# Two graph attention layers on one core: the fourth head's row copied into a PSUM bank, a bias addition a slot earlier, and two inverts moved

## The chip, the cores and the metric

The kernel runs on one core of a Trainium2 chip. The metric is the device time of one execution in microseconds, lower is better. TensorE (PE in the profile) multiplies matrices and writes PSUM only; VectorE (DVE), ScalarE (ACT) and GpSimd (POOL) work elementwise; SyncE (SP) issues the DMA transfers. Each engine works through its own queue in order, and semaphores hold the queues together.

## The reference

There are 16 graphs of 512 nodes with 256 features each, and an adjacency matrix for each. Every graph goes through this:

```python
mask = (adj > 0) | eye(N)
def gat_layer(x, W, a_src, a_dst, bias):      # H heads of F features
    xl = x @ W
    e = leaky_relu(asrc[:, None] + adst[None, :], 0.2)   # source and target scores of each head
    attn = softmax(where(mask, e, -1e9), over sources)
    return attn.T @ xl + bias
h = elu(gat_layer(x, W1, ...))        # layer 1: 4 heads of 128, concatenated
h = gat_layer(h, W2, ...)             # layer 2: one head of 256
x = layernorm(x + h)
Wh = x @ W3                           # layer 3: scores e[i, j] from Wh, masked, softmax over i
x = layernorm(x + leaky(attention @ Wh))
```

## The kernel before, in words

The nodes of a graph (called a batch here) lie in four blocks of 128 partitions. The work of a batch is cut into units: four heads of layer 1 (kind "h", index 0 to 3), layer 2 ("L2") and layer 3 ("L3"). A software pipeline takes one unit per slot and six slots (`SLOTS`) per batch: slot g is slot pos = g % 6 of batch n = g // 6. Position 0 holds layer 3 of batch n-3, positions 1 to 4 the four heads of batch n, position 5 layer 2 of batch n-1. The last layer 3 units come behind the loop. Each engine's block has the same loop over g, and the order of its queue is written out by hand there; nothing plans it.

A unit passes through these steps, over several slots:

- `tops` (line 983, VectorE) finds for each target the greatest source score under the mask, as four calls of 128 x 512, one per block of targets. It adds the transposed mask `mask_t` (bfloat16, SBUF) and the row of source scores, the same on all partitions, and takes the maximum. For the heads of batches from 2 on (`by_dma`) this row is `a_rows[:, index]` in SBUF, which SyncE spreads by DMA (`spread_scores`, 341). For other units TensorE writes it into PSUM bank `bA` (`sources_row`, 514), where it waits for the maxima of the bank's user before (`u.ahead`).
- `shifted_targets` (996, VectorE) makes from the maxima the column `b_t`, in two operations of 128 x 4, `low` (1005) and `b_t` (1010).
- `targets_row` (525, TensorE) spreads b_t over bank bB, as the matmuls of L511.
- `leaky` and `exps` (ScalarE) write the weights into `att`; `keep_edges` (1032, VectorE) takes out the missing edges, in place.
- `attend` (601, TensorE) multiplies by the values, in two halves. It is issued in the slot behind that of its unit.
- `invert` (1020, VectorE) waits for each half of a head's attention and takes the reciprocals of the sums, `normalize` (802, ScalarE) scales with them, `elu_exp` (811, ScalarE) and `elu` (1013, VectorE, tile y) do the elu. TensorE turns y, ScalarE takes its high part, and `low_part` (1027, VectorE, tile y_lo) the rest.

Beside the units run the values of batch n+1 (`values_1`, whose input x_lo is VectorE's, line 1051), the values of layers 2 and 3, the layer norms, and the masks. GpSimd does the bias of layer 2 (`add_bias_2`, 440, 128 x 1024, in slot pos 3, behind the fourth head's b_t), the last residual (`residual_2`, 462, 128 x 1024), the diagonal of the mask (`set_diag`, 456) and the scalings of the last norm (`norm_2`, 425, four of 128 x 256), each for some batch of the pipeline.

In VectorE's loop (line 1226 on) a slot's order is: invert the head of two slots before, maxima and targets of the next unit, the extras of the position, keep_edges of this unit, low part of the head of three slots before, elu of the head of two slots before.

Of the kernel before, what the change touches and what calls it, by code (L numbers as in the profile page):

```python
# [10 lines left out]
ALU = mybir.AluOpType  # L11
# [3 lines left out]
LOWEST = -3.0e38  # L15
# [5 lines left out]
SLOTS = 6  # L21


class Unit:


    def __init__(self, kind, batch, index, slot):
        self.kind = kind
        self.batch = batch
        self.index = index  # L30
        self.slot = slot
        self.row = kind != "L3"

        self.by_dma = kind == "h" and batch >= 2


def gat_kernel(nc, x, adj, W1, as1, ad1, b1, W2, as2, ad2, b2, W3, a3, out):
    B, N, D = x.shape
    HF = W1.shape[1]
    H, F = as1.shape  # L40
# [31 lines left out]
        u.u = i  # L72
    for i, u in enumerate(u for u in units.values() if u.row):
        u.r = i
    spreading = [u for u in units.values() if not u.by_dma]
    for i, u in enumerate(spreading):
        u.a, u.ahead = i, spreading[i - 1] if i else None

    pieces = 0
    for u in units.values():  # L80
# [9 lines left out]
    with ExitStack() as ctx:  # L90
# [6 lines left out]
        def sem(name):  # L97
            return ctx.enter_context(nc.semaphore(name))
# [124 lines left out]
        x1t_ready = sem("x1t_ready")  # L223
        val3_ready = sem("val3_ready")
        exp3_done = sem("exp3_done")
        act3_ready = sem("act3_ready")

        mask_made = sem("mask_made")
# [65 lines left out]
        def a_col(u, b):  # L294
            if u.kind == "h":
                c = HC + u.index % 2
                return val1[u.batch % 2][:, b, u.index // 2, c:c + 1]
            return val2[:, b, 0:1] if u.kind == "L2" else val3[u.batch % 2][:, b, 0:1]
# [16 lines left out]
        def _(sp):  # L315
# [25 lines left out]
            def spread_scores(n):  # L341

                sp.wait_ge(a_stored, 16 * H * (n - 1))
                for h in range(H):
                    if n > 2:
                        sp.wait_ge(top_done, (units[SLOTS * (n - 1) + 1 + h].u + 1) * NB)
                    sp.dma_start(a_rows[:, h], a_dram[h].rearrange("(o n) -> o n", o=1).to_broadcast([P, N]))\
                        .then_inc(a_spread[h], 16)

# [48 lines left out]
        def _(pool):  # L398
# [18 lines left out]
            def norm_scale(m, which, moments_sem, var_sem, rstd_sem):  # L417
                pool.wait_ge(moments_sem, (m + 1) * NB)
                nc.gpsimd.tensor_scalar(var_eps[:, which], moments[:, which, :, 1], EPS, 1.0, ALU.add, ALU.mult)\  # L419
                    .then_inc(var_sem, 1)  # L420
                pool.wait_ge(var_sem, m + 1)
                nc.gpsimd.tensor_tensor(rstd[:, which], var_eps[:, which], neg_half[:], ALU.pow).then_inc(rstd_sem, 1)
                pool.wait_ge(rstd_sem, m + 1)
# [16 lines left out]
            def add_bias_2(m):  # L440
                if m == 0:
                    pool.wait_ge(bias2_ready, 1)
                pool.wait_ge(x_loaded[m % 4], (m // 4 + 1) * 16)
                pool.wait_ge(xt_turned, (m + 1) * KD)
                nc.gpsimd.tensor_tensor(x_in[m % 4][:], x_in[m % 4][:], bias2[:].unsqueeze(1).to_broadcast([P, NB, DO]),
                                        ALU.add).then_inc(xb_done, 1)
# [23 lines left out]
            for g in range(LAST):  # L470
                n, pos = divmod(g, SLOTS)
                if pos == 0 and 0 <= n - 3:
                    scale_3(n - 3)
                if pos == 2 and 0 <= n - 2 < B:
                    norm_scale(n - 2, 0, moments1, var1, rstd1)
                if pos == 2 and 0 <= n - 2 < B:
                    pool.wait_ge(x1n_done, (n - 1) * NB)
                if pos == 2 and 0 <= n - 3 < B:
                    residual_2(n - 3)
                if pos == 2 and 0 <= n + 1 < B:  # L480
                    set_diag(n + 1)
                if pos == 3 and 0 <= n - 1 < B:

                    pool.wait_ge(b_t_ready, units[SLOTS * n + H].r + 1)
                    add_bias_2(n - 1)
                if pos == 4 and 0 <= n - 3:
                    norm_2(n - 3)
            add_bias_2(END)
# [284 lines left out]
        def _(act):  # L773
# [43 lines left out]
            def high_part(u):  # L817
# [2 lines left out]
                    act.wait_ge(val2_done, u.batch * NB)  # L820
                nc.scalar.copy(y_hi[:, u.index], bU[u.turn_use % 4][:]).then_inc(y_hi_ready, 1)

            def x_out(n):
                for k in range(KD):
                    act.wait_ge(xt_turned, n * KD + k + 1)
                    nc.scalar.copy(x_hi[:, k], g_bank(k)).then_inc(x_hi_ready, 1)
# [64 lines left out]
            for g in range(LAST + 1):  # L891
                n, pos = divmod(g, SLOTS)
                if n == 0:
                    first_heads(g)
                    continue
                this, older, oldest = units.get(g), head_at(g - 2), head_at(g - 3)
                third, second, batch = 0 <= n - 2 < B, 0 <= n - 1 < B, 0 <= n + 1 < B
                third_layer = units.get(g - 2) if pos == 2 else None
                if this:
                    leaky(this, (0, 1))  # L900
                if third_layer:
                    third_out(third_layer, 0)
                if older:
                    normalize(older)
                if pos == 5 and n + 2 < B:
                    x_out(n + 2)
                if pos == 0 and batch:
                    values_1_out(n + 1, 0)
                if this:
                    leaky(this, (2, 3))  # L910
                if pos == 2 and batch:
                    values_1_out(n + 1, 3)
                if pos == 3 and second:
                    values_2_out(n - 1, (2, 3))
                if pos == 4 and third:
                    values_3_out(n - 2, (0, 1))
                if this:
                    exps(this)
                if pos in (0, 1) and batch:
                    values_1_out(n + 1, pos + 1)  # L920
                if third_layer:
                    third_out(third_layer, 1)
                if pos == 2 and second:
                    values_2_out(n - 1, (0, 1))
                if pos == 3 and third:
                    x1_out(n - 2)
                if oldest:
                    high_part(oldest)
                if pos == 4 and third:
                    values_3_out(n - 2, (2, 3))  # L930
                if older:
                    elu_exp(older)
# [41 lines left out]
        def _(dve):  # L974
# [7 lines left out]

            def tops(u):

                if u.by_dma:
                    dve.wait_ge(a_spread[u.index], 16 * (u.batch - 1))
                else:
                    dve.wait_ge(arow_done, u.a + 1)
                if u.kind == "h" and u.index == 0:
                    dve.wait_ge(mt_loaded, (u.batch + 1) * NB * 16)  # L990
                for b in range(NB):
                    nc.vector.tensor_tensor_reduce(junk[:, b] if u.row else att[u.slot % 3][:, b], mask_t[u.batch % 4][:, b],  # L992
                                                   a_rows[:, u.index] if u.by_dma else bA[:], 1.0, a_col(u, b) if u.row else LOWEST, ALU.add, ALU.max,
                                                   top[u.u % 2][:, b:b + 1]).then_inc(top_done, 1)

            def shifted_targets(u):
# [130 lines left out]

            def tops_by_targets(u):

                dve.wait_ge(arow_done, u.a + 1)  # L1130
                for b in range(NB):
                    col = slice(b, b + 1)
                    nc.vector.tensor_tensor_reduce(att[u.slot % 3][:, b], mask_t[u.batch % 4][:, b], bA[:], 1.0, LOWEST,
                                                   ALU.add, ALU.max, top[u.u % 2][:, col]).then_inc(top_done, 1)
                    dve.wait_ge(top_done, u.u * NB + b + 1)
                    nc.vector.scalar_tensor_tensor(low[:, col], top[u.u % 2][:, col], -1.0, b_cols(u)[:, col], ALU.mult, ALU.max)\
                        .then_inc(low_done, 1)
                    dve.wait_ge(low_done, u.u + b + 1)
                    nc.vector.scalar_tensor_tensor(b_t3[:, col], top[u.u % 2][:, col], TOP, low[:, col], ALU.subtract,
                                                   ALU.min, reverse0=True).then_inc(b_t3_ready, 1)  # L1140
# [85 lines left out]
            for g in range(LAST + 1):  # L1226
# [3 lines left out]
                    continue  # L1230
                this, after, older, oldest = units.get(g), units.get(g + 1), head_at(g - 2), head_at(g - 3)
                last_head = head_at(g - 4) if pos == 2 else None
                if older and older is not final_head:
                    invert(older)
                if g == LAST:
                    tops(thirds[END - 2])
# [19 lines left out]
                    norm_stats(n - 3, 1, res2, res2_done, 2, stats2, moments2)  # L1256
                if this and this.row:
                    keep_edges(this)
                if oldest and pos != 1:
                    low_part(oldest)  # L1260
                if older:
# [63 lines left out]
```

## Time and profile before

| | |
|---|---|
| median of 3 runs | 930.41 us (929.71 to 932.02) |
| profiled execution | 932.84 us, of which the span of the trace is 930.9 |
| TensorE busy | 852.8 us, 92% of the span |
| VectorE busy | 785.3 us, 84% |
| ScalarE busy | 689.8 us, 74% |
| GpSimd busy | 294.4 us, 32% |
| mean granted TensorE clock | 0.989 of full speed |
| chain that ended last | PE 50%, DVE 27%, ACT 13%, issue 9% |

A timeline row gives the start in us from the span's start, the duration in us, the engine, the line of the kernel, the operation, the tile written and those read, their shapes, and the count of merged instructions. Brackets at its end give how long the engine was idle before it and what released it ("issue" where the profile shows no one). Starts and ends of successive instructions overlap a little, since they are pipelined. Buffer numbers are left out of tile names: `att` is one of three.

### The profile page before, as it was taken

To read this page: it belongs to the slowest core of one execution; us is meant where nothing else is said; L and a number is where in the kernel's file an instruction comes from. 1 tells how busy PE (TensorE), PEld (TensorE's weight loads), DVE (VectorE), ACT (ScalarE), POOL (GpSimd) and SP (SyncE) were. 2 spreads that over 40 slices of the span, in tenths; PEclk is the share of its full clock that TensorE was granted. 3 is DMA by queue.
4 is the path that set the end of the run, shared out by engine and by line. 5 is a ranking of instruction groups with operands and counts; after the bars stand their busy time and mean duration, and the time that the engine had idled before them with its cause. 6 is when DMAs were issued, how large, how long until landed. Compare 5 with 4: busy or idle time off the path is not lost.

```text
span 930.9 us, 16958 instructions
## 1 busy us (share of the span) xinstructions
PE 852.8 (92%) x5996; PEld 791.0 (85%) x5996; DVE 785.3 (84%) x1922; ACT 689.8 (74%) x1288; POOL 294.4 (32%) x244
## 2 busy tenths in 40 slices
PE   6787889999999999999999999999999999989986
PEld 5787779888989888898988889898888989879875
DVE  6766797989897998989899898989989898898666
ACT  2666759779686877968788796878879687797753
POOL 0000101234342623434262342326224242433512
PEclk9898999999999999999999999999999999999999
DMA  9122131311313131121313113231321311100002
GB/s 247 42 74 64 46 91 47 91 46 43 81 60 91 47 113 46 40 75 68 92 46 109 51 35 80 69 92 46 111 49 35 81 69 24 46 24 1 24 0 68
DMA packets 100378, 59.80 MB, mean 64 GB/s; under 512 B 66244, under 2 KB 84804, under 8 KB 100296
## 3 DMA queue, kind: packets, MB, share of 16 engines
q1 hardware_dynamic: 100296, 58.73, 23.1%
q8 instruction: 49, 0.80, 0.5%
q14 instruction: 33, 0.27, 0.2%
HBM read 41.82 MB, written 8.50 MB: 54 GB/s over the span
## 4 chain that ended last, share of the span: by engine, by line
PE 50%; DVE 27%; ACT 13%; issue 9%; another core or an unknown queue 0%; DMA 0%; POOL 0%; DVEq 0%; SPq 0%; POOLq 0%; ACTq 0%
PE bUU L573 10%; DVE junk L992 10%; PE bUU L562 8%; PE bG L645 8%; PE bG L663 8%; PE bUU L551 7%; DVE y L1017 4%; PE bB L511 3%; ACT x L807 3%; DVE y_lo L1029 2%; ACT att L780 2%; DVE stats L1082 2%; DVE att L1039 2%; ACT att L795 2%; ACT att L792 2%
## 5 line engine op out<-in xcount | busy, mean ns | idle before, releaser
L551 PE MATMUL bUU<-val,att 128*128 128x129 f32 x2048 | 249.4, 275 | 0.8 <-DVE att L1043 0.8
L551 PEld LDWEIGHTS bUU<-val,att 128*128 128x128 f32 x2048 | 241.3, 192 | 3.1 <-issue 1.3
L780 ACT ACTIVATE att<-bB,val 128x512 f32<-128x512 f32 x320 | 202.4, 704 | 5.2 <-PE bB L511 5.2
L1043 DVE SCALAR_TENSOR_TENSOR att<-mask_n,att 128x2048 f32<-128x2048 bf16 x64 | 153.6, 2399 | 50.9 <-ACT att L795 50.9
L992 DVE CUSTOM_DVE_ANT_0 junk<-mask_t,a_rows,val 128x512 bf16<-128x512 bf16 x224 | 189.7, 901 | 0.0
L562 PE MATMUL bUU<-val,att 128*128 128x257 f32 x480 | 113.2, 384 | 16.0 <-ACT x L807 13.1
L795 ACT ACTIVATE att<-att 128x2048 f32<-128x2048 f32 x64 | 123.4, 1929 | 0.6
L562 PEld LDWEIGHTS bUU<-val,att 128*128 128x128 f32 x480 | 87.8, 190 | 33.1 <-ACT x L807 18.8
L573 PE MATMUL bUU<-val3s,att 128*128 128x256 f32 x480 | 108.3, 379 | 0.2 <-DVE res L1073 0.2
L419 POOL TENSOR_SCALAR var_eps<-moments 128x4 f32<-128x4 f32 x29 | 32.3, 1115 | 235.8 <-DVE moments L1085 235.8
L807 ACT ACTIVATE x<-bUU,zinv 128x128 f32<-128x128 f32 x256 | 73.2, 369 | 45.1 <-DVE zinv L1023 45.1
L848 ACT COPY val<-bG 128x524 f32<-128x524 f32 x62 | 37.3, 602 | 87.2 <-PE bG L663 87.2
L573 PEld LDWEIGHTS bUU<-val3s,att 128*128 128x128 f32 x480 | 90.0, 190 | 12.3 <-DVE res L1073 0.6
L453 POOL TENSOR_SCALAR val3s<-val,z3inv 128x256 f32<-128x256 f32 x60 | 49.1, 832 | 137.8 <-DVE z3inv L1060 134.7
L511 PE MATMUL bB<-ident,b_t 128*128 128x128 f32 x320 | 51.4, 284 | 34.1 <-DVE b_t L1010 31.8
L645 PE MATMUL bG<-w_hi,y_hi 128*128 128x258 f32 x256 | 75.2, 294 | 0.3 <-DVE y_lo L1029 0.3
L511 PEld LDWEIGHTS bB<-ident,b_t 128*128 128x128 f32 x320 | 35.3, 139 | 44.6 <-DVE b_t L1010 42.1
L663 PE MATMUL bG<-w_hi,x_hi 128*128 128x262 f32 x248 | 72.7, 293 | 0.0
L663 PE MATMUL bG<-w_lo,x_hi 128*128 128x262 f32 x248 | 72.6, 293 | 0.0
L663 PE MATMUL bG<-w_hi,x_lo 128*128 128x262 f32 x248 | 72.5, 292 | 0.0
L645 PE MATMUL bG<-w_hi,y_lo 128*128 128x258 f32 x256 | 72.3, 282 | 0.0
L645 PE MATMUL bG<-w_lo,y_hi 128*128 128x258 f32 x256 | 72.2, 282 | 0.0
(127 smaller groups left out, 1743.5 us busy)
## 6 DMA issues: line engine op xcount, KB each, us to landing
adj_in<-in_adj_dram SPq DMA_DIRECT2D x16, 1024.0 KB, 5.9
a_rows<-a_rows_dram SPq DMA_DIRECT2D x56, 256.0 KB, 3.9
x_in<-in_x_dram SPq DMA_DIRECT2D x16, 512.0 KB, 6.7
out_dram<-act SPq DMA_DIRECT2D x14, 512.0 KB, 2.9
mask_t<-mask_n SPq DMA_TRANSPOSE x64, 2.5
a_rows_dram<-val SPq DMA_DIRECT2D x56, 2.0 KB
att<-in_L_gnn_W_dram SPq DMA_DIRECT2D x4, 128.0 KB, 3.2
val<-in_L_gnn_W_dram SPq DMA_DIRECT2D x1, 512.0 KB, 7.4
```

Source lines behind the costliest of these rows:

```text
L453: nc.gpsimd.tensor_scalar(val3s_of(m, b), val3[m % 2][:, b, 2:DX], z3inv[:, b:b + 1], 1.0, ALU.mult, ALU.mult)\
L511: ins = nc.tensor.transpose(bank[:, b * P:(b + 1) * P], column(b).to_broadcast([P, P]), ident[:])
L551: ins = nc.tensor.matmul(to[:, (d % 2) * FX:(d % 2 + 1) * FX], p[:, s, d * P:(d + 1) * P], val1[u.batch % 2][:, s, u.index // 2, values], ...
L562: ins = nc.tensor.matmul(to[:, 0:DO + 1], p[:, s, d * P:(d + 1) * P], val2[:, s, 2:DX + 1], start=(s == 0), stop=(s == NB - 1))
L573: ins = nc.tensor.matmul(to[:, d * DO:(d + 1) * DO], p[:, j, (2 * i + d) * P:(2 * i + d + 1) * P], val3s[:, j], start=(j == 0), stop=(j == ...
L645: ins = nc.tensor.matmul(g_bank(b % 2)[:, 0:DX], left[:, k, nodes], right[:, k], start=(k == 0 and i == 0), stop=(k == KH - 1 and i == 2))
L663: ins = nc.tensor.matmul(to, left[:, k, nodes], right[:, k, g], start=False, stop=(k == KD - 1 and i == 2))
L780: nc.scalar.activation(p[:, b], bB[:], ACT.Prelu, bias=a_col(u, b), alpha=SLOPE)\
L795: nc.scalar.activation(flat(p), flat(p), ACT.Exp).then_inc(exp_done, 1)
L807: nc.scalar.activation(x1[u.h % 2][:, d * P:(d + 1) * P], bU[u.use[d // 2] % 4][:, (d % 2) * FX:(d % 2) * FX + F], ACT.Copy, scale=zinv[u. ...
L992: nc.vector.tensor_tensor_reduce(junk[:, b] if u.row else att[u.slot % 3][:, b], mask_t[u.batch % 4][:, b], a_rows[:, u.index] if u.by_dma ...
L1043: nc.vector.scalar_tensor_tensor(flat(p), mask_n[u.batch % 3][:, 0:NB * N], BIG, flat(p), ALU.add, ALU.min)\
```

## The change

Three things change. First, the row of the fourth head (index 3) of batches from 2 on is copied from `a_rows` in SBUF into bank bA by ScalarE, in slot pos 2, between the leaky operations of the second head and the copy of the values of the next batch; VectorE's maxima read bA. The bank's order of users takes the fourth heads in, and SyncE waits for the copy, not for the maxima, before it spreads the next row over this part of `a_rows`. Second, GpSimd's bias addition moves from slot pos 3 to pos 2, between the scale of the first norm and the residual, and waits for the third head's b_t instead of the fourth's. Third, the inverts of the third and fourth heads no longer open the slots pos 5 and pos 0; they stand at the end of slots pos 4 and pos 5, behind keep_edges and ahead of the low part. The other inverts stay.

```diff
-        self.by_dma = kind == "h" and batch >= 2
+        self.by_dma = kind == "h" and batch >= 2
+        self.banked = self.by_dma and index == 3
@@
-    spreading = [u for u in units.values() if not u.by_dma]
+    spreading = [u for u in units.values() if not u.by_dma or u.banked]
     for i, u in enumerate(spreading):
         u.a, u.ahead = i, spreading[i - 1] if i else None
+        u.turned = len([v for v in spreading[:i] if not v.banked])
@@ SyncE, spread_scores
-                        sp.wait_ge(top_done, (units[SLOTS * (n - 1) + 1 + h].u + 1) * NB)
+                        if h == H - 1:
+                            sp.wait_ge(arow_copied, n - 2)
+                        else:
+                            sp.wait_ge(top_done, (units[SLOTS * (n - 1) + 1 + h].u + 1) * NB)
@@ GpSimd
                 if pos == 2 and 0 <= n - 2 < B:
                     norm_scale(n - 2, 0, moments1, var1, rstd1)
+                if pos == 2 and 0 <= n - 1 < B:
+                    pool.wait_ge(b_t_ready, units[SLOTS * n + 3].r + 1)
+                    add_bias_2(n - 1)
...
-                if pos == 3 and 0 <= n - 1 < B:
-                    pool.wait_ge(b_t_ready, units[SLOTS * n + H].r + 1)
-                    add_bias_2(n - 1)
@@ ScalarE
+            def row_into_bank(u):
+                act.wait_ge(a_spread[u.index], 16 * (u.batch - 1))
+                act.wait_ge(top_done, (u.ahead.u + 1) * NB)
+                nc.scalar.copy(bA[:], a_rows[:, u.index]).then_inc(arow_copied, 1)
...
                 if this:
                     leaky(this, (2, 3))
+                if pos == 2 and n >= 2:
+                    row_into_bank(units[g + 2])
                 if pos == 2 and batch:
                     values_1_out(n + 1, 3)
@@ VectorE, tops (tops_by_targets likewise waits for u.turned)
-                if u.by_dma:
+                if u.banked:
+                    dve.wait_ge(arow_copied, u.batch - 1)
+                elif u.by_dma:
                     dve.wait_ge(a_spread[u.index], 16 * (u.batch - 1))
                 else:
-                    dve.wait_ge(arow_done, u.a + 1)
+                    dve.wait_ge(arow_done, u.turned + 1)
...
-                                                   a_rows[:, u.index] if u.by_dma else bA[:], 1.0, ...
+                                                   a_rows[:, u.index] if u.by_dma and not u.banked else bA[:], 1.0, ...
@@ VectorE, the loop
-                if older and older is not final_head:
+                if older and older.index < 2 or g == SLOTS:
                     invert(older)
...
                 if this and this.row:
                     keep_edges(this)
+                if pos in (4, 5) and g < LAST - 1:
+                    invert(head_at(g - 1))
                 if oldest and pos != 1:
                     low_part(oldest)
                 if older:
                     elu(older)
```

## Rows read from the trace of the kernel before

**Rows 1.** Busy us by engine in one batch's stretch, with granted clock and DMA

```profile
400.40:454.90 54.50, 51.89 (x374) 48.48 (x373) 48.21 (x116) 42.69 (x81) 21.14 (x15) 1.00 0.24 68
```

**Rows 2.** TensorE's timeline: start, us, operation, [idle before, releaser]

```profile
417.00 0.65 PE L511 MATMUL bB<-ident,b_t 128*128 128x128 f32 x4 [1.10 <-issue]
...
425.32 0.65 PE L511 MATMUL bB<-ident,b_t 128*128 128x128 f32 x4 [0.60 <-DVE b_t L1010]
...
427.55 1.95 PE L551 MATMUL bUU<-val,att 128*128 128x129 f32 x16
...
429.34 0.60 PE L511 MATMUL bA<-ident,val 128*128 128x128 f32 x4
...
434.87 0.36 PE L660 MATMUL bG<-bias,ones_r 128*128 128x262 f32 x1
...
439.41 2.00 PE L562 MATMUL bUU<-val,att 128*128 128x257 f32 x8 [0.86 <-ACT x L807]
```

**Rows 3.** VectorE's timeline in the same stretch

```profile
403.98 0.16 DVE L1010 SCALAR_TENSOR_TENSOR b_t<-top,low 128x4 f32<-128x4 f32 x1
...
411.34 2.29 DVE L992 CUSTOM_DVE_ANT_0 junk<-mask_t,a_rows,val 128x512 bf16<-128x512 bf16 x1
...
413.56 1.63 DVE L992 CUSTOM_DVE_ANT_0 junk<-mask_t,a_rows,val 128x512 bf16<-128x512 bf16 x1
...
416.78 0.16 DVE L1010 SCALAR_TENSOR_TENSOR b_t<-top,low 128x4 f32<-128x4 f32 x1
...
416.86 2.29 DVE L1043 SCALAR_TENSOR_TENSOR att<-mask_n,att 128x2048 f32<-128x2048 bf16 x1
...
420.04 1.88 DVE L1017 SCALAR_TENSOR_TENSOR y<-e,x 128x512 f32<-128x512 f32 x1 [0.89 <-ACT e L815]
...
426.85 2.29 DVE L1043 SCALAR_TENSOR_TENSOR att<-mask_n,att 128x2048 f32<-128x2048 bf16 x1
...
429.66 0.68 DVE L1017 SCALAR_TENSOR_TENSOR y<-e,x 128x512 f32<-128x512 f32 x1
...
430.41 0.67 DVE L992 CUSTOM_DVE_ANT_0 att<-mask_t,bA 128x512 f32<-128x512 bf16 x1
...
433.50 1.22 DVE L1053 TENSOR_TENSOR x_lo<-bG,x_hi 128x1024 fp32r<-128x1024 f32 x1
...
434.99 2.36 DVE L1039 SCALAR_TENSOR_TENSOR att<-mask_n,att 128x1024 f32<-128x1024 bf16 x2 [0.27 <-ACT att L792]
...
441.61 0.16 DVE L1010 SCALAR_TENSOR_TENSOR b_t<-top,low 128x4 f32<-128x4 f32 x1
```

**Rows 4.** L992, the row maximum, by operands: ns min/median/max, first and last start

```profile
L992 DVE CUSTOM_DVE_ANT_0 junk<-mask_t,a_rows,val x224: 728/748/2289, 115.9 to 847.1; 128x512 bf16<-128x512 bf16 x112
...
L992 DVE CUSTOM_DVE_ANT_0 junk<-mask_t,bA,val x96: 720/739/748, 25.0 to 885.0; 128x512 bf16<-128x512 bf16 x96
```

**Rows 5.** GpSimd's timeline in the same stretch

```profile
410.68 2.39 POOL L467 TENSOR_TENSOR res<-act,x1n 128x1024 f32<-128x1024 f32 x1 [8.80 <-DVE x1n L1093]
...
413.04 1.60 POOL L459 TENSOR_TENSOR mask_n<-mask_n,ident_big 128x512 bf16<-128x512 bf16 x1
...
417.02 4.34 POOL L445 TENSOR_TENSOR x_in<-x_in,bias 128x1024 f32<-128x1024 f32 x1 [2.37 <-issue]
...
426.95 2.24 POOL L419 TENSOR_SCALAR var_eps<-moments 128x4 f32<-128x4 f32 x1 [5.59 <-DVE moments L1085]
...
430.41 4.84 POOL L428 TENSOR_SCALAR act<-res,moments,rstd 128x256 f32<-128x256 f32 x4
```

**Rows 6.** ScalarE's timeline in the same stretch

```profile
404.37 0.60 ACT L848 COPY val<-bG 128x524 f32<-128x524 f32 x1 [1.26 <-PE bG L663]
...
422.10 1.14 ACT L807 ACTIVATE x<-bUU,zinv 128x128 f32<-128x128 f32 x4 [0.93 <-DVE zinv L1023]
...
424.77 1.97 ACT L795 ACTIVATE att<-att 128x2048 f32<-128x2048 f32 x1
```

**Rows 7.** GpSimd's residual addition over the whole span, as in rows 4

```profile
L467 POOL TENSOR_TENSOR res<-act,x1n x13: 2372/2394/2397, 192.6 to 842.9; 128x1024 f32<-128x1024 f32 x13
```

More of the change, by code:

```diff
@@ L225, in gat_kernel @@
         exp3_done = sem("exp3_done")
+        arow_copied = sem("arow_copied")
         act3_ready = sem("act3_ready")
@@ L992, in tops @@
                     nc.vector.tensor_tensor_reduce(junk[:, b] if u.row else att[u.slot % 3][:, b], mask_t[u.batch % 4][:, b],
-                                                   a_rows[:, u.index] if u.by_dma else bA[:], 1.0, a_col(u, b) if u.row else LOWEST, ALU.add, ALU.max,
+                                                   a_rows[:, u.index] if u.by_dma and not u.banked else bA[:], 1.0, a_col(u, b) if u.row else LOWEST, ALU.add, ALU.max,
                                                    top[u.u % 2][:, b:b + 1]).then_inc(top_done, 1)
@@ L1128, in tops_by_targets @@
             def tops_by_targets(u):
-                dve.wait_ge(arow_done, u.a + 1)
+                dve.wait_ge(arow_done, u.turned + 1)
                 for b in range(NB):
```

## The prediction

> **What bounds the kernel now.** I read three kinds of view in this order: the busy time of one stretch, the engines' timelines over that stretch, and the durations of VectorE's row maximum by its operands. The stretch 400.4 to 454.9 us is one batch in the steady part, and TensorE is busy 51.9 of its 54.5 us at the full clock (1.00, 2.4 GHz), VectorE 48.2, ScalarE 42.7 [rows 1]. So TensorE is the bound, and a change can win only the time in which it stands still, unless it makes it stand still more. In the batch TensorE has three waits: 1.10 us before the targets' row of the fourth head (start 417.00), 0.60 before that of the second layer (425.32), 0.86 inside the second layer's attention (439.41) [rows 2]. The idle column counts from end to start, while groups that don't wait overlap by 427.55 + 1.95 - 429.34 = 0.16 us [rows 2], so each costs that much more: 1.27, 0.77 and 1.02. Beside them, TensorE's start at 434.87 follows VectorE's x_lo, done at 433.50 + 1.22 = 434.72 [rows 2, 3], so x_lo paces it there with no wait to speak of. The ceiling of any gain is therefore about 3.2 us a batch.
>
> The first wait is for the fourth head's b_t, which VectorE has done at 416.78 + 0.16 = 416.94 [rows 3]; the view calls its releaser "issue", but TensorE starts 0.06 us behind that. It is late because of the row maxima before it: the first took 2.29 and the second 1.63 us [rows 3], where the median of the form is 0.75 [rows 4]. Meanwhile GpSimd ran its residual addition (410.68 to 413.07) and the diagonal (413.04 to 414.64) [rows 5]. The maxima end when those end: one engine holds something and the other waits. The same is seen at 420.04, where the elu (y) took 1.88 against GpSimd's bias addition, which ended at 421.36, and that addition took 4.34 because keep_edges, 416.86 to 419.15, had started first [rows 3, 5].
>
> **The change part by part.** *The row in the bank.* The maximum from bank bA took 720 to 748 ns in all 96 cases, while the form from a_rows reaches 2289 [rows 4]. The third layer's first maximum, from bA as well, ran at 430.41 in 0.67 us under GpSimd's scalings, which began at the same 430.41 [rows 3, 5]. So the fourth head's maxima lose (2.29 - 0.75) + (1.63 - 0.75) = 2.4 us, and b_t comes at 414.5 (414.7 if its two small operations, which read SBUF twice, wait for the diagonal). TensorE is free at 417.00 - 1.27 = 415.73, so the first wait goes whole: TensorE 1.27 sooner. The other bank users stand in VectorE's own order, and bA is free: the third layer's maxima end by 434 of the batch before, the second layer's row needs it only after the fourth head.
>
> *ScalarE's copy.* It stands after the second head's leaky operations, and ahead of the copy at 404.37 ScalarE idles 1.26 us for TensorE [rows 6]. No row shows a copy from SBUF to PSUM. The nearest is that same copy of 524 columns from PSUM to SBUF, 0.60; from below it can't cost less than nothing, from above the exponential over four times as many columns, in SBUF alone, took 1.97 [rows 6]. I take 0.6, which the idle time hides; at 1.97 it would put 0.7 us a batch on ScalarE ahead of the second head's exponential. VectorE's new wait on it is over 7 us before the maxima at 411.34. SyncE's queue waits for the copy where it waited for the maxima, so the spreading of the next row is never later, and nothing behind it is.
>
> *GpSimd's bias a slot sooner.* It now starts at the third head's b_t, done at 403.98 + 0.16 = 404.14 [rows 3], and needs 4.34 less what it waited, 419.15 - 417.02, that is 2.3 us; it ends near 406.6. VectorE's next operation is keep_edges, which waits for ScalarE's exponential, and that starts some 0.5 behind the copy at 404.37 and takes 1.9, to 406.8 [rows 6]. So the bias lies in VectorE's idle time. Residual and diagonal follow at 410.68 as before. What it frees is y, which took 0.68 at 429.66: 1.88 - 0.68 = 1.20 us [rows 3].
>
> *What comes next in the batch.* TensorE's 1.27 brings x1 turned, ScalarE's copies and y's input 1.27 sooner; y starts at 418.77 and its end is 1.27 + 1.20 = 2.47 sooner. The second layer's maxima and b_t move with it, more than TensorE's 1.27 + 0.77, so the second wait goes too: TensorE 2.04 sooner. ScalarE's wait of 0.93 at 422.10 goes [rows 6]; it is then 1.27 + 0.93 and an overlap of 0.13 sooner, 2.33. So the fourth head's exponential ends at 424.77 + 1.97 - 2.33 = 424.41, and keep_edges runs 424.5 to 426.8 (before: 426.85 to 429.14 [rows 3]).
>
> *The inverts moved ahead.* For the third head VectorE now stands, behind keep_edges, until TensorE's attention is done: 427.55 + 1.95 - 2.04 = 427.46 [rows 2]. That is a new wait of 0.6 us, and low part, y and the third layer's maxima are queued behind it. The low part, an operation over as many columns as y, takes 0.6 to the start of the next, so y would start at 428.17. GpSimd's scalings start 430.41 - 429.14 = 1.27 us behind the end of keep_edges [rows 3, 5], so at 428.1. This is a near tie. I take it that GpSimd is first; y then waits for the first of four scalings, 4.84 / 4 = 1.21 us, until 429.2, and the third layer's maxima start at 429.8 instead of 430.41: 0.6 sooner. x_lo moves with them. TensorE had 2.04 and stands 1.4 us for x_lo. Behind x_lo, VectorE's wait of 0.27 for the exponential [rows 3] goes, so its work is 0.87 sooner from there.
>
> The fourth head's invert moves from behind two operations of 0.6 to ahead of them, which with the 0.87 is 2.1 us sooner; ScalarE's normalizing of the fourth head is then in time and the third wait, 1.02, goes. But TensorE's next need is the next batch's first b_t, at 441.61 + 0.16 = 441.77 before [rows 3], which VectorE brings 0.87 sooner. So TensorE stands once more, and the batch is 0.87 us shorter. From there TensorE leads to the fourth head again (ScalarE's idle time at 404.37 is such a wait), so nothing more is lost or won.
>
> **The sum.** The residual addition runs 13 times, from 192.6 to 842.9 [rows 7]: 13 batches have the collision. 13 x 0.87 = 11.3 us. The batches before them have no residual and no scalings; the new wait on the third head's invert and the earlier bias offset each other there, and I put them at nothing. The last batch, in which fewer things pace TensorE, may give a little more: 11.9 in all. Against the profiled execution (932.84, of which 930.9 is the span) that gives 920.9; the median of the runs shown is 2.4 lower, 930.41, and from it the forecast is 918.5 us.
>
> The one rule I weigh is that of the near tie. The rows show one wait of y that lasts to the end of one GpSimd operation, and a maximum that got in between residual and diagonal: the diagonal's 1.60 and the maximum's 1.63 took turns [rows 3, 5]. The Trainium skill, "SBUF — State Buffer", section "Who interferes with whom", says that a VectorE operation with two SBUF inputs and a GpSimd one that reads SBUF exclude each other for a whole instruction, and that issue order alone decides who waits. By that rule the tie's two ends are one scaling or none, never four; the first gives the sum above, the second the rival A below, and the rule speaks against rival B. The trace agrees with 1.88 for y.
>
> **The rivals.** *A, y is first at the tie.* Then the third layer's maxima start at 428.77, 1.64 sooner. GpSimd's scalings end later and may hold keep_edges of the second layer by some 0.5 us, so 1.4 a batch: 13 x 1.4 = 18.2, 912 us. For it: 0.07 us decides, and the tie may fall differently by batch. Against: the estimate of the tie itself.
>
> *B, VectorE does not get its turn between the four scalings (slower than before).* y, behind the new wait, stands for all 4.84 us, to 432.9; the third layer's maxima start near 433.5, 3.1 later than now, x_lo and TensorE with them; less the 0.27, 2.8 a batch, 13 x 2.8 = 36: 967 us. It decides from the point where y waits for more than 1.9 us, that is, where the maxima start after 430.41 + 0.27: with a second scaling, 1.2 more, the batch is 0.3 longer and the time 934. For it: the four have no wait between them. Against: the turn taken behind the residual.
>
> *C, the bank does not shield the maxima* (the change doesn't do what it says). Then the first wait stays, only y's 1.20 is won, and the invert's wait eats it: 930 us. Against: the 96 unslowed cases of [rows 4].
>
> *D, nothing stands behind the invert.* If the attention is done before keep_edges and the tie is won, TensorE itself is the limit and wins more of the 3.2 us a batch: 2.2 x 13 = 29, 902 us. Against: the third layer's maxima and targets, 433.50 - 430.41 = 3.1 us, stand ahead of x_lo [rows 3].
>
> **How the numbers follow.** The forecast has 0.50, A 0.25, B 0.07 (mostly its small form), C 0.10, D 0.08. The forecast and A hold three quarters, and the unknown copy could put up to 0.7 a batch, 9 us, on the forecast, with a small chance; so the range is 908 to 926. This kernel's measurement tells 0.3% from no change, 2.8 us, so faster means below 927.6: forecast, A and D nearly whole, 0.83. Within 0.3%: 0.10 (C and a dear copy). Slower: 0.07.
>
> **What would show it.** In the changed profile the fourth head's maxima should read bA and take 0.72 to 0.75 each; the bias addition should take 2.3 to 2.4 in every batch, and y at the fourth head's slot 0.68. TensorE's 1.10 and 0.60 waits should be gone, and the 0.86; in their place stand one of some 1.4 us before the L660 matmuls, released by x_lo, and one of some 0.9 before the first head's targets' row. The y under the scalings should take about 1.7. The distance of two residual additions should be 53.6 to 53.7 instead of 54.5. The forecast is wrong if ScalarE's copy takes over 1.26, if y there takes 0.68 (A) or over 3 (B), or if the first wait is still there (C).

## The result, and the profile after

The changed kernel took 906.6 us (median of 4 runs, 904.33 to 908.52) against 930.1 before: a ratio of 0.974 with a 95% interval of 0.972 to 0.977. It is faster by 2.6%, 23.5 us, about twice what I forecast, and 1.4 us below the low end of my range. The profiled execution's span is 904.3 us. One batch's stretch of it, with the columns of [rows 1]:

```profile
388.80:441.40 52.60, 51.21 (x373) 48.56 (x372) 44.47 (x114) 43.03 (x82) 17.83 (x15) 1.00 0.26 62
```

The view counts 373 matmuls where [rows 1] has 374, at the same clock, in a stretch 1.9 us shorter. VectorE is busy 3.7 us less: what has gone is time in which its operations stood under GpSimd. GpSimd, which stood as well, is busy 3.3 less.

The distance of the residual additions, seen over all 13 [rows 7], gives the mean batch between the first and the last of them: (842.9 - 192.6) / 12 = 54.19 us before, and after

```profile
L474 POOL TENSOR_TENSOR res<-act,x1n x13: 2393/2394/2406, 188.5 to 816.6; 128x1024 f32<-128x1024 f32 x13
```

(816.6 - 188.5) / 12 = 52.34. That is 22.2 us over 12 distances. The two profiled spans, 930.9 and 904.3, differ by 26.6, so 4.1 us of the profiles' difference lie ahead of the first residual addition (192.6 against 188.5) and 0.3 behind the last. In the steady batches the distance went from 54.5 to 52.6.

The batch that answers to the one shown before has its residual addition at 399.07 where [rows 5] has 410.68, so 11.61 is to be added to compare. TensorE's timeline at the places of [rows 2], in the new line numbers:

```profile
404.21 0.60 PE L518 MATMUL bB<-ident,b_t 128*128 128x128 f32 x4
...
411.71 0.60 PE L518 MATMUL bB<-ident,b_t 128*128 128x128 f32 x4
...
421.81 0.36 PE L667 MATMUL bG<-bias,ones_r 128*128 128x262 f32 x1 [0.65 <-DVE x_lo L1069]
...
423.60 3.63 PE L569 MATMUL bUU<-val,att 128*128 128x257 f32 x16
...
428.41 0.65 PE L518 MATMUL bB<-ident,b_t 128*128 128x128 f32 x4 [0.74 <-DVE b_t L1026]
```

The three waits of [rows 2] are gone: the targets' rows have no brackets, and the second layer's attention, which was cut in two by 0.86, is one row of 16. In their place stand the two that I forecast, one on x_lo and one on the next batch's first b_t, 0.65 and 0.74 where I had 1.4 and 0.9.

VectorE's timeline of the same batch:

```profile
399.82 0.73 DVE L1008 CUSTOM_DVE_ANT_0 junk<-mask_t,bA,val 128x512 bf16<-128x512 bf16 x1
400.47 0.74 DVE L1008 CUSTOM_DVE_ANT_0 junk<-mask_t,bA,val 128x512 bf16<-128x512 bf16 x1
...
402.80 0.16 DVE L1026 SCALAR_TENSOR_TENSOR b_t<-top,low 128x4 f32<-128x4 f32 x1
...
407.12 0.69 DVE L1033 SCALAR_TENSOR_TENSOR y<-e,x 128x512 f32<-128x512 f32 x1
...
412.78 2.29 DVE L1059 SCALAR_TENSOR_TENSOR att<-mask_n,att 128x2048 f32<-128x2048 bf16 x1
...
415.88 0.17 DVE L1039 RECIPROCAL zinv<-bUU 128x2 f32<-128x2 f32 x1 [0.73 <-PE bUU L558]
...
416.55 0.88 DVE L1033 SCALAR_TENSOR_TENSOR y<-e,x 128x512 f32<-128x512 f32 x1
417.35 0.67 DVE L1008 CUSTOM_DVE_ANT_0 att<-mask_t,bA 128x512 f32<-128x512 bf16 x1
...
420.45 1.21 DVE L1069 TENSOR_TENSOR x_lo<-bG,x_hi 128x1024 fp32r<-128x1024 f32 x1
421.59 2.34 DVE L1055 SCALAR_TENSOR_TENSOR att<-mask_n,att 128x1024 f32<-128x1024 bf16 x2
...
428.19 0.16 DVE L1026 SCALAR_TENSOR_TENSOR b_t<-top,low 128x4 f32<-128x4 f32 x1
```

The maxima from the bank take 0.73 and 0.74 although GpSimd's residual runs beside them, y at 407.12 takes 0.69 where [rows 3] had 1.88, and before the third head's invert VectorE stands 0.73 for TensorE, the new wait. GpSimd and ScalarE there:

```profile
392.71 2.37 POOL L452 TENSOR_TENSOR x_in<-x_in,bias 128x1024 f32<-128x1024 f32 x1 [2.83 <-DVE b_t L1026]
399.07 2.40 POOL L474 TENSOR_TENSOR res<-act,x1n 128x1024 f32<-128x1024 f32 x1 [4.00 <-DVE x1n L1109]
401.43 1.17 POOL L466 TENSOR_TENSOR mask_n<-mask_n,ident_big 128x512 bf16<-128x512 bf16 x1
...
416.34 4.85 POOL L435 TENSOR_SCALAR act<-res,moments,rstd 128x256 f32<-128x256 f32 x4
```

```profile
391.42 0.64 ACT L833 COPY bA<-a_rows 128x512 f32<-128x512 f32 x1
392.84 0.60 ACT L860 COPY val<-bG 128x524 f32<-128x524 f32 x1 [0.78 <-PE bG L670]
```

The bias takes 2.37 for 4.34, the diagonal 1.17 for 1.60 [rows 5]. ScalarE's copy costs 0.64, and it still idles 0.78 behind it. The row that decides my error is y at 416.55: the first scaling had started 0.21 us before it, and y was late by 0.20, not by the rest of that scaling.

The tie between y and the scalings fell this way in 7 of the 13 batches, in which y took 0.88. In the other 6 y was first and took 0.68, and the four scalings took 5.20 to 5.39 instead of 4.85, as in the next batch:

```profile
470.31 0.68 DVE L1033 SCALAR_TENSOR_TENSOR y<-e,x 128x512 f32<-128x512 f32 x1
```

```profile
470.52 5.20 POOL L435 TENSOR_SCALAR act<-res,moments,rstd 128x256 f32<-128x256 f32 x4
```

### The profile page after: what moved, and what is told of

Its sections match the earlier page's. It is cut to its first block, busy times and chain, and to the rows that moved or that the text cites. A ratio compares the mean times of both kernels' runs of the same rounds, so it can differ in the third digit from the quotient of the medians.

```text
span 904.3 us, 16988 instructions
## 1 busy us (share of the span) xinstructions
PE 842.7 (93%) x5996; PEld 789.3 (87%) x5996; DVE 742.3 (82%) x1922; ACT 694.7 (77%) x1302; POOL 266.7 (29%) x244
## 4 chain that ended last, share of the span: by engine, by line
PE 65%; DVE 24%; issue 5%; ACT 4%; another core or an unknown queue 0%; DMA 0%; POOL 0%; SPq 0%; POOLq 0%; DVEq 0%; ACTq 0%
PE bUU L558 16%; PE bUU L580 11%; PE bG L652 10%; DVE junk L1008 8%; PE bG L670 7%; PE bG L640 5%; PE bUU L569 5%; PE bB L518 4%; DVE att L1008 4%; DVE y L1033 2%; DVE att L1055 2%; DVE y_lo L1045 2%; PE bG L631 1%; PE bUU L548 1%; PE bG L667 1%
## 5 line engine op out<-in xcount | busy, mean ns | idle before, releaser
L1059 DVE SCALAR_TENSOR_TENSOR att<-mask_n,att 128x2048 f32<-128x2048 bf16 x64 | 150.0, 2344 | 76.0 <-ACT att L802 73.5
L426 POOL TENSOR_SCALAR var_eps<-moments 128x4 f32<-128x4 f32 x29 | 29.9, 1032 | 317.8 <-DVE moments L1101 317.8
L1008 DVE CUSTOM_DVE_ANT_0 junk<-mask_t,a_rows,val 128x512 bf16<-128x512 bf16 x168 | 116.7, 751 | 0.0
L569 PE MATMUL bUU<-val,att 128*128 128x257 f32 x480 | 110.0, 381 | 3.7 <-DVE att L1055 2.7
L1008 DVE CUSTOM_DVE_ANT_0 junk<-mask_t,bA,val 128x512 bf16<-128x512 bf16 x152 | 104.1, 741 | 4.1 <-PE bA L518 4.1
L460 POOL TENSOR_SCALAR val3s<-val,z3inv 128x256 f32<-128x256 f32 x60 | 39.1, 666 | 128.7 <-DVE z3inv L1076 125.6
```

The source lines that it names most:

```text
L569: ins = nc.tensor.matmul(to[:, 0:DO + 1], p[:, s, d * P:(d + 1) * P], val2[:, s, 2:DX + 1], start=(s == 0), stop=(s == NB - 1))
L1059: nc.vector.scalar_tensor_tensor(flat(p), mask_n[u.batch % 3][:, 0:NB * N], BIG, flat(p), ALU.add, ALU.min)\
```

## The experiments

T1 is my theory, the forecast's chain of steps with y's wait corrected; T2 says that each of the three parts closes one of TensorE's three waits and that they add up. T3, which only the long hold tests, says that y's wait does not reach TensorE. All kernels in the table are built from the changed one. Each ratio is to the kernel before as it ran beside that kernel (930.4 to 932.3 us). "Batch" is the mean distance of the 13 residual additions.

| kernel | median us | ratio to before, interval | batch us |
|---|---|---|---|
| changed, run again | 906.7 | 0.9727 (0.9701 to 0.9752) | |
| bank alone | 906.5 | 0.9731 (0.9715 to 0.9748) | 52.29 |
| bias alone | 917.7 | 0.9852 (0.9835 to 0.9869) | 53.04 |
| inverts alone | 927.5 | 0.9966 (0.9954 to 0.9978) | 54.00 |
| bank and bias | 905.5 | 0.9717 (0.9694 to 0.9740) | 52.14 |
| bias and inverts | 922.5 | 0.9904 (0.9887 to 0.9922) | 53.44 |
| bank and inverts | 904.0 | 0.9701 (0.9682 to 0.9721) | 51.98 |
| long hold | 914.7 | 0.9827 (0.9802 to 0.9852) | 53.22 |
| reordered | 892.5 | 0.9585 (0.9559 to 0.9610) | 51.33 |
| reordered again | 895.3 | 0.9605 (0.9584 to 0.9625) | |

### The bank alone, and the bank with the bias

```diff
 (the changed kernel)
-                if older and older.index < 2 or g == SLOTS:
+                if older and older is not final_head:
                     invert(older)
...
-                if pos in (4, 5) and g < LAST - 1:
-                    invert(head_at(g - 1))
```

For the bank alone the bias addition goes back to slot pos 3 as well.

> Only the fourth head's row goes through the bank; the bias addition stays behind the fourth head's b_t, and the inverts open their slots as before. My theory (T1): the maxima get 2.4 us shorter, so TensorE's waits of 1.27 and 0.77 us both go (b_t of the second layer moves with y, since the bias, which now starts at 414.7, ends before y is ready), and the wait of 1.02 inside the second layer's attention stays: some 2.0 us a batch, 13 batches, 904 us, about as fast as the whole change. Rival T2 (the three parts add up, each closing one of TensorE's three waits): 1.27 a batch, 914 us.

> Row through the bank and bias a slot sooner, inverts as before. T1: VectorE never stands for the third head's attention and x_lo comes without a wait, but the wait of 1.02 for the fourth head's normalizing stays; 2.0 to 2.1 us a batch, 903 to 905 us, not slower than the whole change at 906.6. T2: the inverts close the third wait, so without them 1.02 x 13 = 13 us of the gain are missing: 920 us.

Measured: 906.5 and 905.5. The bank alone gives all of the gain, and taking the moved inverts out of the change costs nothing (905.5 against 906.6 and 906.7, intervals that overlap). T2 falls: it had 914 and 920, and T1 had 904 and 903 to 905. TensorE's waits between 200 and 740 us are, first in the kernel with bank and bias and no moved inverts, then in the changed one (columns: total us, times, longest):

```profile
PE bUU L569 <- ACT x L814: 8.1, 10, 1.0
PE bB L518 <- DVE b_t L1026: 0.5, 1, 0.5
```

```profile
PE bB L518 <- DVE b_t L1026: 9.0, 13, 0.9
PE bG L667 <- DVE x_lo L1069: 5.7, 11, 0.7
```

Without the moved inverts the wait for the fourth head's normalizing stays, 0.8 a batch. With them it is gone, and b_t and x_lo take its place with 14.7 us over 10.3 batches, 1.4 a batch. The moved inverts exchange one wait for two, no shorter together.

### Parts without the bank

```diff
-        self.banked = self.by_dma and index == 3
+        self.banked = False
```

ScalarE's copy and SyncE's wait for it are taken out with it. "no_bank" has bias and inverts as changed; of "bias alone" and "inverts alone" the rest is as before.

> Bias and inverts as changed, but the fourth head's maxima read the row in SBUF as before. T1: the wait of 1.27 for the fourth head's b_t stays; y is 1.2 sooner, TensorE 0.77 sooner behind the second wait; the third head's invert then stands for the attention until 428.7 and leaves 0.2 + 0.27 of it: 0.45 a batch, 924 us. T2: 0.77 + 1.02 a batch: 907 us.

> Only the bias addition a slot sooner. T1: y no longer collides, the second wait of 0.77 goes, nothing else: 0.77 x 13 = 10 us, 920 us. T2: the same 0.77 a batch, 920 us. A third reading, by which all that the kernel gains is VectorE's time (1.2 us of collision a batch): 914 us.

> Only the inverts of the third and fourth heads moved. T1 (the moved invert makes VectorE stand for the third head's attention, and what is queued behind it is late): in the kernel before, the attention ends at 429.50, keep_edges at 429.14; low part, y and the third layer's maxima come 0.4 us later, x_lo with them, of which a wait of 0.27 takes up a part: 0.2 us a batch longer, 933 to 935 us against 931. T2 (the early invert closes the wait of 1.02 a batch): 918 us.

Measured: 922.5, 917.7 and 927.5. The bias alone is worth 1.5%, 13.8 us, and that decides between none of the readings: T1 and T2 both had 10 us, and the third, by which VectorE's 1.2 us of collision a batch are the gain, had 914. In the steady batches the distance fell from 54.5 to 53.2, which is nearer to the third; why it is more than the 0.77 of TensorE's wait was not traced. T1 holds for bias and inverts together (924 forecast), where T2 had 907: the moved inverts cost 4.8 us there. For the inverts alone both missed. They gain a little, 0.3%, not T2's 1.3%, and not the loss of T1. TensorE's rows there show where T1's loss went:

```profile
415.15 0.65 PE L516 MATMUL bB<-ident,b_t 128*128 128x128 f32 x4 [1.10 <-DVE b_t L1022]
...
433.38 0.36 PE L665 MATMUL bG<-bias,ones_r 128*128 128x262 f32 x1 [0.41 <-DVE x_lo L1065]
439.97 0.65 PE L516 MATMUL bB<-ident,b_t 128*128 128x128 f32 x4 [0.73 <-DVE b_t L1022]
...
469.67 0.65 PE L516 MATMUL bB<-ident,b_t 128*128 128x128 f32 x4 [1.10 <-DVE b_t L1022]
```

TensorE waits 0.41 for x_lo, as T1 said, but the wait for b_t, 0.73, only takes the place of the 0.86 for the normalizing. A batch in this part takes 54.52 us, 469.67 less the 415.15 of the same wait one batch earlier, as before the change. The small gain lies outside the steady batches: by the two profiles 1.8 us ahead of the first residual addition (190.8 against 192.6) and 1.5 in the last of the 12 distances (48.4 against 49.9). What makes it there was not traced.

### The bank and the inverts, without the bias's move

> Bank and moved inverts, the bias addition behind the fourth head's b_t as before. T1: once the maxima read the bank, b_t comes 2.4 us sooner and the bias with it, so it ends before y is ready; it only holds keep_edges of the third head for some 0.5 us. The bias's move is then worth next to nothing in the whole change, though it is worth 1.5% alone: 906 to 909 us. T2 (each part closes its own wait): 906.6 + 10 = 917 us.

Measured: 904.0, while the changed kernel took 906.7 beside it (T1 had 906 to 909). The bias's move is worth nothing once the bank is there; whether it costs is open, since the intervals overlap. T2's 917 falls. VectorE's third-head keep_edges takes 2.64 instead of 2.29 beside the later bias, less than the 0.5 I had expected, and it costs nothing that TensorE waits for:

```profile
405.51 2.64 DVE L1059 SCALAR_TENSOR_TENSOR att<-mask_n,att 128x2048 f32<-128x2048 bf16 x1 [1.96 <-ACT att L802]
408.07 0.68 DVE L1033 SCALAR_TENSOR_TENSOR y<-e,x 128x512 f32<-128x512 f32 x1
...
417.15 0.68 DVE L1033 SCALAR_TENSOR_TENSOR y<-e,x 128x512 f32<-128x512 f32 x1
```

```profile
417.25 5.30 POOL L435 TENSOR_SCALAR act<-res,moments,rstd 128x256 f32<-128x256 f32 x4
```

This kernel also shows the tie's other end. Here y, at 417.15, is 0.10 us ahead of the scalings and takes 0.68, in every batch, and a steady batch takes 52.4 us against the changed kernel's 52.6.

### A longer hold at the same place

This kernel leaves out the last norm's scaling of batches 0 to 12 and puts one addition in its place.

```diff
-                for b in range(NB):
-                    nc.gpsimd.tensor_scalar(act3[:, b], res2[:, b], moments[:, 1, b, 0:1], rstd[:, 1, b:b + 1],
-                                            ALU.subtract, ALU.mult).then_inc(y_out_done, 1)
+                nc.gpsimd.tensor_tensor(flat(act3), flat(res2), flat(res2), ALU.add).then_inc(y_out_done, 4)
```

> The whole change, with GpSimd's four scalings of 128 x 256 (the last norm of batches 0 to 12, which is left out) put in one addition of 128 x 1024, whose row in the kernel before is 2.4 us and which there held a maximum for 2.2. T1 (y's wait under GpSimd, which I had put at 1.0 and which was 0.2, is what my sum got wrong, and it goes into x_lo and the batch at its full length): y takes 2.5 to 2.7 where GpSimd is first, the batch is 1.8 longer there: 929 us if that is so in all 13 batches, 918 if in half. Rival T3 (the wait of y does not reach TensorE, and the sum was off elsewhere): 906 us as the whole change, or less, since GpSimd works 2.4 us less a batch.

Measured: 914.7, 8 us more than the changed kernel although GpSimd works less. T3, which had 906 or less, falls. T1 has the direction, but its 918 to 929 is too high. GpSimd and y in one batch:

```profile
420.67 1.89 POOL L434 TENSOR_TENSOR act<-res 128x1024 f32<-128x1024 f32 x1
```

```profile
420.86 2.25 DVE L1031 SCALAR_TENSOR_TENSOR y<-e,x 128x512 f32<-128x512 f32 x1
```

y takes 2.25 where it took 0.88, and TensorE's longest wait for x_lo grows from 0.7 to 1.6. The addition's row was 1.89 long, not the 2.4 I had expected (it reads one tile twice), so y was 1.4 later instead of 1.8, and that in 10 of the 13 batches; the mean batch went from 52.34 to 53.22, the steady one from 52.6 to 53.7. So of 1.4 us that y waits longer, 1.1 reach a steady batch: most of the wait does, and not all of it. That makes my mis-sized term large enough to explain most of the miss.

### The hold, measured alone

Two small kernels of their own leave out the whole computation. ScalarE releases both engines; VectorE does y's operation behind some tiny reciprocals (one in the first kernel; here the second, without its semaphore increments). "Port" below stands for what the two engines exclude each other from:

```python
for i, (kind, late) in enumerate(trials):
    dve.wait_ge(go, i + 1)
    for k in range(late):
        nc.vector.reciprocal(small[:, 2 * k:2 * k + 2], col[:, 0:2])
    nc.vector.scalar_tensor_tensor(y[:], e[:], 1.0, x1[:], ALU.min, ALU.max)
```

> A kernel of its own: ScalarE releases VectorE and GpSimd together, 36 times; VectorE does a tiny reciprocal and then y's operation (128 x 512, two SBUF inputs, 0.68 us alone), GpSimd one of: a memset of two columns; a scaling of 256 columns with two pointer scalars; one with a pointer and an immediate; an addition of 256; an addition of 1024; a scaling of 1024 with two pointer scalars. The rest of the computation is left out. If the port is held for the whole row, as I forecast, y's operation is late by the row less the head start of about 0.2: 1.0 for the scaling of 256. If only while the columns are read: 0.2 to 0.3 for the scaling of 256, though its row is 1.22, and 0.9 or more for that of 1024.

In the first kernel y and GpSimd's scaling or addition started within 0.05 us of each other, and the answer was not the one expected: y was never late against a scaling (0.67 in all 18 cases), while the scaling of 256 took 1.78 instead of 1.22. Against an addition of 256 y took 1.23, but for the first of six, and against one of 1024 2.85. So a scaling does not take the port at its start. The second kernel places y at other points:

> As the kernel that measures the port alone, but y's operation comes 0 to 11 tiny operations behind the release (some 0.1 us apart), twice each, against a scaling of 256 columns with two pointer scalars, one with a pointer and an immediate, an addition of 256, and a scaling of 1024. In the changed kernel y, 0.21 us behind the scaling's start, went on at 0.41 of its 1.22. If the port is held for that part alone, y is late only for starts between about 0.1 and 0.4 us behind the scaling's start, and on time from 0.5; if it were held to the row's end, y would be late up to 1.1.

GpSimd's scalings of 256 columns with two pointer scalars, and VectorE's operation beside each of them, in the same order:

```profile
20.39 1.74 POOL L74 TENSOR_SCALAR scaled<-pin,col 128x256 f32<-128x256 f32 x1 [0.38 <-ACT go_sb L94]
...
24.11 1.22 POOL L74 TENSOR_SCALAR scaled<-pin,col 128x256 f32<-128x256 f32 x1 [0.38 <-ACT go_sb L94]
...
30.50 1.22 POOL L74 TENSOR_SCALAR scaled<-pin,col 128x256 f32<-128x256 f32 x1 [0.38 <-ACT go_sb L94]
...
36.89 1.22 POOL L74 TENSOR_SCALAR scaled<-pin,col 128x256 f32<-128x256 f32 x1 [0.38 <-ACT go_sb L94]
```

```profile
20.53 0.67 DVE L65 SCALAR_TENSOR_TENSOR y<-e,x 128x512 f32<-128x512 f32 x1
...
24.31 0.89 DVE L65 SCALAR_TENSOR_TENSOR y<-e,x 128x512 f32<-128x512 f32 x1
...
30.82 0.77 DVE L65 SCALAR_TENSOR_TENSOR y<-e,x 128x512 f32<-128x512 f32 x1
...
37.34 0.67 DVE L65 SCALAR_TENSOR_TENSOR y<-e,x 128x512 f32<-128x512 f32 x1
```

y started 0.14, 0.20, 0.32 and 0.45 us behind the scaling, and would have gone on without it 0.67 before its end. That puts the release at 24.31 + 0.89 - 0.67 - 24.11 = 0.42, and again at 0.42 for the third. At 0.14 y is first, and the scaling is 0.52 longer. So the port was held from between 0.14 and 0.20 to 0.42 of a row of 1.22 us; the 0.88 of the changed kernel lies on the same line. An addition of 256 columns (row 0.72) blocked y from its start to 0.60: y started 0.04 behind it and took 1.23.

### Reordered

The bank and the bias as changed, the inverts as before, and in slot pos 5 low part and y behind the next maxima:

```diff
 VectorE
-                if oldest and pos != 1:
+                deferred = pos == 5 and g < LAST - 1
+                if oldest and pos != 1 and not deferred:
                     low_part(oldest)
-                if older:
+                if older and not deferred:
                     elu(older)
...
+                if pos == 0 and SLOTS < g < LAST:          # behind tops and shifted_targets
+                    low_part(head_at(g - 4))
+                    elu(head_at(g - 3))
 TensorE, slot pos 0: turn_head(oldest) behind targets_row(after) and values_1 instead of ahead of them
```

> Bank and bias, inverts as before the change; in slot pos 5 VectorE's low part and y move behind the maxima and b_t of the next batch's first head, and TensorE turns y behind that row and the values. T1: the kernel without the moved inverts still waits 0.70 to 1.04 us a batch for the fourth head's normalizing, released by VectorE's invert, and then needs b_t at about the moment it comes; both come 1.2 us sooner, so TensorE waits for neither: about 1.0 a batch, 13 to 14 batches, 892 us. Rival: y and low part, now later, hold TensorE's turning or a bank instead: 903 us or more.

> The reordered kernel beside the changed one: 14 us less, 890 to 895 us. If the gain over the changed kernel was one of chips, it is much smaller here.

> The changed kernel once more, to stand on the same chip as the next two: 905 to 909 us.

Measured: 906.7 for the changed kernel once more, which is 906.6 again. The reordered kernel took 892.5, and 895.3 beside those 906.7 on the same chip, 1.3% less. TensorE in 540 us of it:

```profile
200.00:740.00 540.00, 538.58 (x3896) 507.51 (x3896) 469.71 (x1204) 453.53 (x858) 198.12 (x160) 1.00 0.26 71
```

It stands for 1.4 us in 540, at a granted clock of 1.00. This is the fastest kernel of the study, and in this part little but less TensorE work would make it faster. Its steady batch of 51.2 us is 3.3 below the 54.5 before.

## Why the prediction was wrong

The order of events was right, and most of its times. Adding 11.61 to the rows after: the fourth head's b_t is done at 402.96, that is 414.57 (forecast 414.5). y starts at 418.73 (418.77) and takes 0.69 (0.68). keep_edges of the fourth head starts at 424.39 (424.5). The third head's attention releases VectorE at 427.49 (427.46), y comes at 428.16 (428.17), GpSimd's scaling is ahead of it (427.95, forecast 428.1). The three waits closed, and two others opened where I had them.

The step that failed is the one worded "y then waits for the first of four scalings, 4.84 / 4 = 1.21 us, until 429.2". y waited 0.20 instead of 1.03. I took the row's duration for the time in which the other engine is shut out; the staggered kernel shows that to be 0.42 from the scaling's start. The 0.83 us go straight on: the third layer's maxima at 428.96 instead of 429.8, x_lo at 432.06 after 433.50 before, the next b_t 1.8 sooner instead of 0.87. 13 x 0.83 = 10.8 us, and 918.5 - 10.8 = 907.7, with 906.6 measured.

That the sum then comes so near is in part luck, for other terms were off too and don't stand in it. A steady batch is 1.9 us shorter, where 0.87 + 0.83 is 1.7. Of the 0.2 left, 0.08 is VectorE's wait of 0.27 ahead of keep_edges of the second layer, which cost 0.35: without it the two rows overlap (421.59 after 420.45 + 1.21). The rest was not traced. The batches ahead of the collisions, which I had put at nothing, have 4.1 us in the two profiles, 1.0 of it ahead of the first y (49.8 against 48.8). From the first y to the first residual addition the profiles have 142.8 us before, 139.8 changed, 140.7 with the bias alone, 141.7 with the inverts alone and 142.9 with the bank alone, but 142.5 with bank and bias. So it comes from the bias and the inverts and not from the bank, and how stays open. Behind the last residual addition, where I had one more collision and 0.6 of the tail, 0.3 was gained.

The trace of before had held a hint. One of GpSimd's four scalings of the third layer's values was on at 446.62, when a maximum with two SBUF inputs came:

```profile
446.14 0.91 POOL L453 TENSOR_SCALAR val3s<-val,z3inv 128x256 f32<-128x256 f32 x1
```

```profile
446.62 0.96 DVE L992 CUSTOM_DVE_ANT_0 junk<-mask_t,a_rows,val 128x512 bf16<-128x512 bf16 x1
```

It lost 0.96 - 0.75 = 0.21, so it went on at 446.83, 0.22 ahead of the end of the scaling's row. It is no more than a hint: this form, with one pointer and an immediate, takes 0.47 where nothing disturbs it, and its row here is nearly twice that. I had sized a scaling by additions, which do shut out nearly to their end.

The rule weighed, of the Trainium skill's "SBUF — State Buffer", "Who interferes with whom", holds here in that y waited for one operation or none, never for four. "For the whole instruction" holds for the additions within 0.12 us of the row (0.60 of 0.72) and fails for the scalings (0.42 of 1.22), if the row is taken as the instruction. That issue order alone decides fails close to a tie, if it is taken from the rows: a scaling that started 0.14 ahead still lost the port.

Smaller points. Three sums of the forecast are slightly off: the three waits add up to 3.06 and not 3.2 (the reordered kernel won 3.3 a steady batch), the bias without its wait is 4.34 - 2.13 = 2.21 and not 2.3 (it took 2.37), and 1.21 behind 428.1 is 429.3 and not 429.2. None of them moves the forecast by more than 2 us. The 13 batches as the place of the gain: right for most of it, 22.2 of the 26.6 us between the two profiles. ScalarE's copy at 0.6: right, 0.64, hidden. Rival A (y first) has the better number, 912, and its mechanism was there in 6 of the 13 batches, though not in the one shown. It doesn't explain the miss: the five steady batches in which GpSimd was first take 52.6 us, and the 6 take 52.3 to 53.5. The three longer ones of the 6 have one more wait for b_t (0.91, 0.47 and 0.17), and the other three are 0.2 to 0.3 shorter than 52.6, as y's missing wait of 0.20 would have it. I had also charged A 0.5 for keep_edges of the second layer, which the rows don't show (2.35 with y first, 2.34 behind, 2.36 before). B, C and D did not come. What the forecast did not say, because it summed the change as a whole, is that the inverts' move brings nothing: its own step had them cost a wait of 0.6 and close one of 1.02, and behind both stood the b_t that cancels them.

## What to carry to other kernels

When two engines shut each other out, measure how long from a stretched row of the operation that waits, not from the length of the row that blocks: here a scaling let go at a third of its row, and an addition only near its end. When a change has parts, ask of each what TensorE waits for next if that part is left out: here one part by itself gave as much as all three, the second was worth 1.5% alone and nothing beside the first, and the third exchanged waits. And read the waits that are left, for they name the next edit: with the inverts back in their places, two operations moved behind the maxima gave a further 1.3%.

## What the runs showed of the hardware

- A row maximum that reads PSUM and one SBUF tile is not slowed by GpSimd (0.73 to 0.75 under an addition that made the same maximum with two SBUF inputs take 2.29).
- GpSimd's scaling with two pointer scalars leaves the port free at the start of its row and through most of it: taken between 0.14 and 0.20, released at 0.42 of 1.22 us for 256 columns. An addition held it from the start to 0.60 of 0.72.
- ScalarE's copy of 128 x 512 from SBUF to PSUM took 0.64 us.
